# Storing the sums early and adding the expert outputs by accumulating DMAs, in a two-layer attention and mixture-of-experts kernel

## The chip, the cores and the metric

The kernel runs on one core of a Trainium2 chip. The metric is the device time in microseconds, median of several runs of one launch. The engines are TensorE (PE, with its weight loads as PEld), VectorE (DVE), ScalarE (ACT), GpSimd (POOL) and SyncE (SP). SP issues the plain DMAs and POOL the indirect ones, whose row addresses come from a tile of numbers.

## The reference

The input is x with 16 batches of 512 tokens of 128 numbers. Two layers follow; each adds an attention and a feed-forward part to x.

```
xn = layernorm(x)
x = x + cosformer_attention(xn) + moe0(xn)          # 16 experts, top 4, and 2 shared ones
xn = layernorm(x)
x = x + rope_attention(xn) + moe1(xn)
# moe1: 8 experts, each token goes to the one with the highest probability
route = softmax(xn @ router_w + router_b)
for e in range(8):
    a, g = split(xn @ w1[e])                         # w1[e]: 128 x 1024
    y = (silu(a) * g) @ w2[e]                        # w2[e]: 512 x 128
    out = where(argmax(route) == e, y, out)
out = out * max(route)
```

The change touches the last line, the addition of `moe1` to x, and the way in which the result reaches memory.

## The kernel before, in words

**Order.** Each engine runs its own program, and semaphores tie them together. All programs are cut from one list of stages. `placed` gives each stage of a batch a position by hand, in units of which a batch has 20 (`NS`); `stages` sorts all of them by position. So a stage's place in the list decides what stands ahead of it on its engine. The lists `FIRST`, `SECOND` and `ATTENTION` are laid down for each of the 16 batches, and batches overlap. The list `LAST` counts from the last batch.

**Sorting.** As each batch is routed, POOL writes its normalized rows (`sort`, one indirect DMA for 128 rows) into the memory tensor `xs`, each row at a slot of its expert. A row is 129 numbers, 128 values and the token's number. SP later fills the end of each expert's region with 128 rows of zeros marked -1 (`pads`).

**Expert tiles.** `tables` works out which 128 rows and which expert each of 72 tiles has (64 full ones, and up to 8 for the remainders). A tile n has these stages, 1.3 units apart from tile to tile:
- `load` (SP, L1294 and L1295): reads the row address from a table, and brings the tile into one of 4 buffers, `xsb[n % 4]`. The load of tile n+4 waits until tile n has been transposed (`xsT_mm`) and POOL has its row numbers (`rows`).
- `rows` (POOL, L1181 to L1185): three small operations that turn the token numbers into row addresses, with the padding sent to spare rows.
- `turned` (PE L620, ACT L763): the transpose, and its copy to SBUF. `staged` (ACT L757) copies the expert's first weights.
- `hidden` (PE L628, ACT L769, DVE L1076 and L1079): the first product and the gate.
- `outputs` (PE L639): the second product. ACT L774 copies it from PSUM to `ysb`, and POOL L1192 writes it by an indirect DMA to the rows of its tokens in the memory tensor `ys`.

In PE's program the transpose of tile n+1 stands ahead of the first product of tile n and of the second product of tile n-1. The first 20 or so tiles run among the attention of the last batch; the rest run alone.

**The end.** x, with attention and the first layer added, stays in SBUF in the tile `X` until the end (DVE L1021, stage `out`, makes the last addition per batch and counts `x2`). When all rows have arrived in `ys`, SP reads them back in four parts (L1314). DVE multiplies each by the tokens' highest probabilities `pmax` (L1101) and adds it to `X` (L1102), and SP stores it (L1317).

The functions that the change touches follow.

Of the kernel before, what the change touches and what calls it, by code (L numbers as in the profile page):

```python
# [7 lines left out]
ALU = mybir.AluOpType  # L8
# [25 lines left out]
NTAB = NTILE + U  # L34
# [8 lines left out]
K_ID, K_NEG, K_BD, K_TRI, K_ONE, K_SINB, K_COSB, K_RC, K_RS, K_SC, K_BH, K_T, K_E, K_J, K_EYE = range(15)  # L43
WIDTHS = [P, 4 * P, P, P, P, L, L, L, L, 2 * NT, H, NT, 3 * E1 + 1, NTAB, P // 2]
# [3 lines left out]
def constants():  # L48
# [29 lines left out]
    put(K_J, np.arange(NTAB)[None, :])  # L78
    return t
# [30 lines left out]
def placed(**places):  # L110
# [46 lines left out]
    out=[24.55])  # L157
# [3 lines left out]
LAST = [(-19.5, "w1", 0), (-4.5, "w2", 0), (-13, "spares", 0)] + [(-12.4 + 1.2 * k, "tables", k) for k in range(6)]  # L161
# [85 lines left out]
def once(names):  # L247
# [12 lines left out]
    "max heads x2 tables rowzero silu glu chain final "  # L260

    "fills kept ones var0 var1 rstd0 rstd1 qs gated rotated noaT spare nextspare rows xsorted spare_rows "

    "d_x d_w d_restx d_gate d_gates d_relayq d_relayk d_relayed d_sorted d_w1 d_w2 d_pad d_out"
) + [f"d_xs{u}" for u in range(U)] + [f"d_ys{u}" for u in range(U)] + ["d_y"]
# [6 lines left out]
def place(nc, ctx, io):  # L272
# [10 lines left out]
    m.pmax = sb("pmax", [P, B * NT])  # L283
    m.zeros = sb("zeros", [P, D + 1])
# [8 lines left out]
    m.yg = flow[:, :].rearrange("p (t d) -> p t d", d=D)  # L293
# [24 lines left out]
    with ExitStack() as side:  # L318
# [20 lines left out]
        m.xn = [sb(f"xn{n}", [P, NT, D + n], where=side) for n in range(2)]  # L339
# [46 lines left out]
    m.ysb = sb("ysb", [P, U, D])  # L386
# [19 lines left out]

Q = 4
# [384 lines left out]
def vector_program(nc, m, s, order, work):  # L792
# [154 lines left out]
    def expert(b, i):  # L947
# [3 lines left out]
        then(dve.tensor_reduce(m.pmax[:, b * NT:(b + 1) * NT], m.p1[:, :, :], AX_X, ALU.max))  # L951
# [73 lines left out]
    def tables(_, k):  # L1025
# [33 lines left out]
        else:  # L1059
# [4 lines left out]
            then(dve.tensor_scalar(jr[:, 3, :], jr[:, 2, :], float(E1 * CAP), None, ALU.min))  # L1064
# [31 lines left out]

    n = B * NT // Q
    for q in range(Q):
        y, xq = m.yg[:, q * n:(q + 1) * n, :], m.X[:, q * n:(q + 1) * n, :]
        dve.wait_ge(s[f"d_xs{q}"], 16 * (NTILE // U + 2))  # L1100
        then(dve.tensor_tensor(y, y, m.pmax[:, q * n:(q + 1) * n].unsqueeze(2).to_broadcast([P, n, D]), ALU.mult))  # L1101
        dve.tensor_tensor(xq, xq, y, ALU.add).then_inc(s["final"], 1)  # L1102


def pool_program(nc, m, s, order, work):
# [94 lines left out]
    pool.memset(m.zeros[:, D:], -1.0)  # L1200
# [22 lines left out]
def sync_program(nc, m, s, io, order):  # L1223
# [85 lines left out]
    n = B * NT // Q  # L1309
    for u in range(U):  # L1310
# [4 lines left out]
    for q in range(Q):  # L1315
# [65 lines left out]
```

## Time and profile before

| | us |
|---|---|
| median of 3 runs | 1367.89 |
| lowest and highest | 1367.87, 1368.88 |
| span of the profiled execution | 1371.5 |
| PE busy in it | 1209.3 (88%) |
| DVE busy | 991.5 (72%) |
| ACT busy | 912.8 (67%) |
| POOL busy | 692.6 (50%) |

The profile is one execution. Its span, from the first to the last instruction, is its own time, and it is 3.6 us longer than the median. All positions in time below are counted from the span's start. Busy shares are a mean over stages with different limits, so each stage has to be read by itself.

### The profile page before, as it was taken

To read this page: it belongs to the slowest core of one execution; us is meant where nothing else is said; L and a number is where in the kernel's file an instruction comes from. 1 tells how busy PE (TensorE), PEld (TensorE's weight loads), DVE (VectorE), ACT (ScalarE), POOL (GpSimd) and SP (SyncE) were. 2 spreads that over 40 slices of the span, in tenths; PEclk is the share of its full clock that TensorE was granted. 3 is DMA by queue.
4 is the path that set the end of the run, shared out by engine and by line. 5 is a ranking of instruction groups with operands and counts; after the bars stand their busy time and mean duration, and the time that the engine had idled before them with its cause. 6 is when DMAs were issued, how large, how long until landed. Compare 5 with 4: busy or idle time off the path is not lost.

```text
span 1371.5 us, 28942 instructions
## 1 busy us (share of the span) xinstructions
PE 1209.3 (88%) x10216; PEld 700.1 (51%) x10216; DVE 991.5 (72%) x2378; ACT 912.8 (67%) x1233; POOL 692.6 (50%) x1093
## 2 busy tenths in 40 slices
PE   2675999999999999999999999999986999899990
PEld 1342445445454545454454545454432476799990
DVE  2163888888888988888888989888868462344545
ACT  1141777778687868777786877787773667577760
POOL 6324455554536464554545464655543345466760
PEclk9898999999999999999999999999996799999995
DMA  7323505050524416060515335060615210111118
GB/s 224 63 57 64 111 19 115 20 103 27 96 53 71 91 32 120 11 115 20 103 34 88 72 52 105 19 120 14 111 37 171 74 29 25 31 48 50 50 48 250
DMA packets 80300, 100.90 MB, mean 74 GB/s; under 512 B 8800, under 2 KB 56672, under 8 KB 79776
## 3 DMA queue, kind: packets, MB, share of 16 engines
q1 hardware_dynamic: 75680, 89.85, 29.9%
q0 software_dynamic: 4480, 9.22, 2.3%
q8 instruction: 84, 1.38, 0.5%
q14 instruction: 56, 0.46, 0.1%
HBM read 73.50 MB, written 25.01 MB: 72 GB/s over the span
## 4 chain that ended last, share of the span: by engine, by line
PE 63%; DVE 20%; issue 5%; ACT 4%; POOL 4%; DMA 3%; ACTq 0%; SPq 0%; DVEq 0%; POOLq 0%
PE PS L628 9%; PE PS L595 8%; PE PS L440 7%; PE PS L484 7%; PE PS L561 5%; PE PS L639 4%; PE PS L580 4%; PE PS L423 4%; DVE xn L824 3%; PE PS L434 2%; DVE nm L985 2%; DMA early<-gate_rows 2%; PE PS L462 2%; PE PS L570 2%; DVE ra L933 1%
## 5 line engine op out<-in xcount | busy, mean ns | idle before, releaser
L735 ACT ACTIVATE flow<-PS 128x1024 f32<-128x1024 f32 x320 | 321.2, 1028 | 129.4 <-PE PS L580 112.1
L1146 POOL TENSOR_SCALAR_AFFINE_SELECT flow<-flow 128x256 f32<-128x256 f32 (+1 forms) x448 | 191.0, 444 | 374.3 <-ACT flow L735 371.7
L595 PE MATMUL PS<-flow 128*32 128x512 f32 (+3 forms) x2048 | 181.2, 455 | 6.2 <-POOL flow L1146 6.2
L985 DVE TENSOR_REDUCE nm<-PS 128x2 f32<-128x1024 f32 x128 | 154.6, 1220 | 42.3 <-PE PS L549 38.9
L1133 POOL TENSOR_TENSOR early<-early 128x512 f32<-128x512 f32 x128 | 160.7, 1270 | 20.9 <-DMA early<-gate_rows 20.0
L484 PE MATMUL PS<-early,down 128*128 128x512 f32 x288 | 151.8, 637 | 18.4 <-POOL early L1133 17.9
L726 ACT COPY qp<-PS 2x1024 f16<-2x1024 f16 x128 | 128.5, 1004 | 51.0 <-PE PS L570 49.8
L440 PE MATMUL PS<-xnT,up 128*128 128x512 f32 x288 | 152.6, 625 | 3.7 <-DVE at L908 3.4
L987 DVE TENSOR_REDUCE nm<-PS 128x2 f32<-128x768 f32 x128 | 121.6, 950 | 32.4 <-PE PS L549 32.3
L628 PE MATMUL PS<-xsT,w1s 128*128 128x128 f32 x1152 | 141.5, 276 | 3.0 <-DVE act L1079 2.9
L1076 DVE SCALAR_TENSOR_TENSOR tanh<-tanh,PS 128x512 f32<-128x512 f32 x72 | 49.5, 687 | 130.0 <-ACT tanh L769 130.0
L561 PE MATMUL PS<-kp,qp 34*128 34x512 f16 (+3 forms) x1024 | 121.3, 305 | 17.5 <-DVE nm L988 7.8
L628 PEld LDWEIGHTS PS<-xsT,w1s 128*128 128x128 f32 x1152 | 134.5, 192 | 4.3 <-issue 4.1
L667 ACT ACTIVATE early<-PS 128x512 f32<-128x512 f32 x144 | 84.5, 597 | 54.5 <-PE PS L440 53.7
L580 PE MATMUL PS<-qp,kp 34*128 34x512 f16 (+3 forms) x1024 | 114.7, 306 | 5.5 <-ACT flow L735 1.9
L1192 POOL DMA_INDIRECT ys<-ysb,rowu x72 | 76.6, 1063 | 83.2 <-ACT ysb L774 39.2
L561 PEld LDWEIGHTS PS<-kp,qp 34*128 34x128 f16 x1024 | 38.2, 94 | 114.9 <-issue 43.9
L757 ACT COPY w1s<-early 128x1024 f32 x72 | 75.2, 1045 | 23.7 <-issue 23.7
L595 PEld LDWEIGHTS PS<-flow 128*32 128x32 f32 x2048 | 48.6, 110 | 82.1 <-issue 71.1
L580 PEld LDWEIGHTS PS<-qp,kp 34*128 34x128 f16 x1024 | 35.3, 94 | 107.9 <-issue 70.4
L991 DVE TENSOR_REDUCE nm<-PS 128x4 f32<-128x1024 f32 x64 | 78.0, 1219 | 16.3 <-PE PS L549 16.2
L1157 POOL DMA_INDIRECT xs<-xn,slotu x64 | 66.4, 1037 | 39.5 <-DVE slotu L976 29.1
(178 smaller groups left out, 2263.3 us busy)
## 6 DMA issues: line engine op xcount, KB each, us to landing
early<-gate_rows SPq DMA_DIRECT2D x32, 1024.0 KB, 10.8
qp<-relay_q SPq DMA_DIRECT2D x64, 128.0 KB
kp<-relay_k SPq DMA_DIRECT2D x64, 128.0 KB
xsb<-xs SPq DMA_DIRECT2D x76, 64.5 KB, 1.8
relay_k<-qkh SPq DMA_DIRECT2D x32, 128.0 KB, 2.3
early<-in_w SPq DMA_DIRECT2D x1, 4096.0 KB, 14.8
out_y<-X SPq DMA_DIRECT2D x4, 1024.0 KB, 7.9
relay_q<-qkh SPq DMA_DIRECT2D x16, 128.0 KB, 2.3
```

Source lines behind the costliest of these rows:

```text
L440: pe.matmul(ps, m.up[:, c * P:(c + 1) * P], m.xnT[0][:, :], start=True, stop=True).then_inc(s["up_mm"], 1)
L484: pe.matmul(m.acc, m.down[:, c, :], m.hid[:, c, :], start=(c == 0), stop=False)
L561: pe.matmul(ps[:, k, o:o + w], head(m.qp, b, 4 * g + h, slice(qt * P, (qt + 1) * P)), head(m.kp, b, 4 * g + h, slice(0, w)), start=(o == 0 ...
L580: ins = pe.matmul(ps[:, k, o:o + L - kt * P], head(m.kp, b, h, slice(kt * P, (kt + 1) * P)), head(m.qp, b, h, slice(kt * P, L)), start=(o ...
L595: ins = pe.matmul(m.PS[32 * j:32 * j + 32, m.PV, kt * P:], m.vst[b % 2][:, kt, 4 * g + j, :], m.pt[:, r, k * L + o:k * L + o + L - kt * P] ...
L628: ins = pe.matmul(m.PS[:, at + i // FC, i % FC * P:(i % FC + 1) * P], m.w1s[:, n % WS, i * P:(i + 1) * P], m.xsT[:, n % 2, :], start=True, ...
L726: ins = act.copy(m.qp[b % 2][at:at + 2, 2 * g:2 * g + 2, :], ps[at:at + 2, :, :])
L735: act.activation(m.pt[:, n % RING, :], m.PS[:, i:i + 2, :].rearrange("p k c -> p (k c)"), ACT.Exp, scale=1.0 / SCALE).then_inc(s["exp"], 1)
L985: dve.tensor_reduce(nm[:, 3, 2 * n:2 * n + 2], ps, AX_X, ALU.max, negate=True).then_inc(s["max"], 1)
L987: dve.tensor_reduce(nm[:, 2, 2 * n - 4:2 * n - 2], ps[:, :, 0:3 * P], AX_X, ALU.max, negate=True)
L1133: pool.tensor_tensor(m.hid[:, c, :], m.hid[:, c, :], m.gates[:, c - 1, :], ALU.mult).then_inc(s["gated"], 1)
L1146: ins = pool.affine_select(part, part, [[0, part.shape[1]], [1, P]], ALU.is_ge, nothing, base=0, channel_multiplier=-1)
```

## The change

- `xs` rows have 130 numbers: 128 values, the number of the output row, and the highest probability, which DVE writes there at routing. `pmax` is gone.
- The padding rows carry numbers of spare rows at the end of the output and a probability of 0. The spare rows are given a value by one DMA of zeros; the caller cuts them off. So `rows` on POOL is one copy (L1167) instead of three operations, and the stage `spares` is gone.
- The output of a tile is multiplied by the probability as ACT takes it from PSUM, and goes to a slot of `X`, which is free again by then.
- A stage `store` per batch, on SP, writes x of the batch to the output as soon as the sum is made.
- A stage `scatter` on POOL adds a tile's rows to the output rows in memory by an indirect DMA that accumulates. It stands at `max(tile(n + 1) + 0.4, 25 + 0.4 * n)`. The first waits for all stores.
- The load of tile n+4 also waits for tile n's copy from PSUM.
- The read back, the multiplications and additions at the end and the last stores are gone.

```
-LAST = [(-19.5, "w1", 0), (-4.5, "w2", 0), (-13, "spares", 0)] + [(-12.4 + 1.2 * k, "tables", k) for k in range(6)]
+LAST = [(-19.5, "w1", 0), (-4.5, "w2", 0)] + [(-12.4 + 1.2 * k, "tables", k) for k in range(6)]
+    store=[24.8])
+LAST += [(max(tile(n + 1) + 0.4, 25 + 0.4 * n), "scatter", n) for n in range(NTILE)]
...
     def outputs(_, n):
         act.wait_ge(s["yo_mm"], n + 1)
-        act.wait_ge(s[f"d_ys{n % U}"], 16 * (n // U + 1))
-        act.copy(m.ysb[:, n % U, :], wk(("outputs", 0, n))[:, 0:D]).then_inc(s["ycopy"], 1)
+        if n == 0:
+            act.wait_ge(s["d_out"], 16 * (B - 2))
+        if n == FIRSTS:
+            act.wait_ge(s["d_last"], 16 * 2)
+        if n == B * NT:
+            act.wait_ge(s["d_head"], 16 * E1)
+        act.activation(m.X[:, n % (B * NT), :], wk(("outputs", 0, n))[:, 0:D], ACT.Copy,
+                       scale=m.xsb[:, n % U, D + 1:D + 2]).then_inc(s["ycopy"], 1)
...
     def rows(_, n):
         u = n % U
         pool.wait_ge(s[f"d_xs{u}"], 16 * (n // U + 1))
-        pool.wait_ge(s[f"d_ys{u}"], 16 * (n // U + 1))
-        if n:
-            pool.wait_ge(s["nextspare"], n)
-        pool.tensor_scalar(m.isno[:, :], m.xsb[:, u, D:D + 1], 0.0, m.spare[:, 0:1], ALU.is_lt,
-                           ALU.mult).then_inc(s["spare"], 1)
-        pool.wait_ge(s["spare"], n + 2)
-        pool.tensor_scalar(m.rowu[:, u:u + 1], m.isno[:, :], m.xsb[:, u, D:D + 1], None, ALU.add).then_inc(s["rows"], 1)
-        pool.tensor_scalar(m.spare[:, :], m.spare[:, :], float(P), None, ALU.add).then_inc(s["nextspare"], 1)
-
-    def outputs(_, n):
-        u = n % U
+        if n == 0:
+            pool.wait_ge(s["tables"], 1)
+        pool.tensor_copy(m.rowu[:, n:n + 1], m.xsb[:, u, D:D + 1]).then_inc(s["rows"], 1)
+
+    def scatter(_, n):
+        if n == 0:
+            pool.wait_ge(s["d_out"], 16 * (B - 2))
+            pool.wait_ge(s["d_last"], 16 * 2)
+            pool.wait_ge(s["d_spare"], 16)
         pool.wait_ge(s["ycopy"], n + 1)
         pool.wait_ge(s["rows"], n + 1)
         alone()
-        pool.indirect_dma_start(m.ys_d, bass.IndirectOffsetOnAxis(ap=m.rowu[:, u:u + 1], axis=0),
-                                m.ysb[:, u, :], None).then_inc(s[f"d_ys{u}"], 16)
+        pool.indirect_dma_start(m.rows_d, bass.IndirectOffsetOnAxis(ap=m.rowu[:, n:n + 1], axis=0),
+                                m.X[:, n % (B * NT), :], None,
+                                compute_op=ALU.add).then_inc(s["d_head" if n < E1 else "d_added"], 16)
...
     def pads(_, i):
         sp.wait_ge(s["rowzero"], 1)
+        marks = const(m, K_SP).rearrange("p (j c) -> p j c", c=2)
         for e in range(E1):
             row = sp.value_load(m.ti[0:1, 0, e:e + 1], min_val=0, max_val=E1 * CAP - P)
-            sp.dma_start(m.xs_d[bass.ds(row, P), :], m.zeros[:, :]).then_inc(s["d_pad"], 16)
-        sp.dma_start(m.xs_d[E1 * CAP:E1 * CAP + P, :], m.zeros[:, :]).then_inc(s["d_pad"], 16)
+            sp.dma_start(m.xs_d[bass.ds(row, P), 0:D], m.zeros[:, 0:D]).then_inc(s["d_pad"], 16)
+            sp.dma_start(m.xs_d[bass.ds(row, P), D:], marks[:, e, :]).then_inc(s["d_pad"], 16)
+        last = m.xs_d[E1 * CAP:E1 * CAP + E1 * P, :].rearrange("(j p) c -> p j c", p=P)
+        sp.dma_start(last[:, :, 0:D], m.zeros[:, 0:D].unsqueeze(1).to_broadcast([P, E1, D])).then_inc(s["d_pad"], 16)
+        sp.dma_start(last[:, :, D:], marks[:, E1:, :]).then_inc(s["d_pad"], 16)
     def load(_, n):
         if n >= U:
             sp.wait_ge(s["xsT_mm"], n - U + 1)
             sp.wait_ge(s["rows"], n - U + 1)
+            sp.wait_ge(s["ycopy"], n - U + 1)
+    def store(b, i):
+        if b == 0:
+            sp.dma_start(m.spare_d, m.zeros[:, 0:D].unsqueeze(1).to_broadcast([P, NPAD, D])).then_inc(s["d_spare"], 16)
+        sp.wait_ge(s["x2"], b + 1)
+        sp.dma_start(m.out_d[:, b], m.X[:, b * NT:(b + 1) * NT, :]).then_inc(s["d_out" if b < B - 2 else "d_last"], 16)
...
-    for u in range(U):
-        sp.wait_ge(s[f"d_ys{u}"], 16 * (NTILE // U + 1))
-    for q in range(Q):
-        src = m.ys_d[q * n * P:(q + 1) * n * P, :].rearrange("(t p) d -> p t d", p=P)
-        sp.dma_start(m.yg[:, q * n:(q + 1) * n, :], src).then_inc(s[f"d_xs{q}"], 16)
-    for q in range(Q):
-        sp.wait_ge(s["final"], q + 1)
-        sp.dma_start(m.out_d[:, q * B // Q:(q + 1) * B // Q].rearrange("p b t d -> p (b t) d"),
-                     m.X[:, q * n:(q + 1) * n, :]).then_inc(s["d_out"], 16)
-    sp.wait_ge(s["d_out"], 16 * Q)
+    sp.wait_ge(s["d_out"], 16 * (B - 2))
+    sp.wait_ge(s["d_last"], 16 * 2)
+    sp.wait_ge(s["d_spare"], 16)
+    sp.wait_ge(s["d_head"], 16 * E1)
+    sp.wait_ge(s["d_added"], 16 * (NTILE - E1))
```

On POOL, before, each expert tile has the same four instructions: three for its row numbers and the indirect DMA of the tile two before it. At tile 20 they are:

```order
L1192 DMA ys<-ysb,rowu 18176x128 [waits s_ycopy,s_rows]
L1181 TENSOR_SCALAR isno<-xsb,spare 128x1 [waits s_nextspare,s_d_ys3,s_d_xs3]
L1184 TENSOR_SCALAR rowu<-isno,xsb 128x1 [waits s_spare]
L1185 TENSOR_SCALAR spare<-spare 128x1
L1192 DMA ys<-ysb,rowu 18176x128 [waits s_ycopy,s_rows]
L1181 TENSOR_SCALAR isno<-xsb,spare 128x1 [waits s_nextspare,s_d_ys0,s_d_xs0]
```

Now the row copies of tiles 16 to 20 stand alone, and the scatters of the tiles from 0 on follow in groups between the next copies:

```order
L1167 CAST rowu<-xsb 128x1 [waits s_d_xs3]
L1167 CAST rowu<-xsb 128x1 [waits s_d_xs0]
L1177 DMA out_y<-X,rowu 10240x128 [waits s_ycopy,s_rows,s_d_spare,s_d_out,s_d_last]
L1177 DMA out_y<-X,rowu 10240x128 [waits s_ycopy,s_rows] x3
L1167 CAST rowu<-xsb 128x1 [waits s_d_xs1]
L1177 DMA out_y<-X,rowu 10240x128 [waits s_ycopy,s_rows] x3
L1167 CAST rowu<-xsb 128x1 [waits s_d_xs2]
L1177 DMA out_y<-X,rowu 10240x128 [waits s_ycopy,s_rows] x3
```

What moved: the DMA of a tile has left its place two tiles behind. The copies of tiles 21 to 28 stand behind 4, 7, 10, 13, 17, 20, 23 and 26 scatters, and from there on one copy follows each scatter.

On SP, before, only loads stand here, each behind two waits:

```order
L1294 TENSOR_LOAD ji [waits s_rows,s_xsT_mm]
L1294 ISA x2
L1295 ISA
L1295 DMA xsb<-xs 128x129
L1294 TENSOR_LOAD ji [waits s_rows,s_xsT_mm]
```

Now they have three, and the store of the last batch stands between the loads of tiles 23 and 24:

```order
L1284 TENSOR_LOAD ji [waits s_ycopy,s_rows,s_xsT_mm]
L1284 ISA x2
L1285 ISA
L1285 DMA xsb<-xs 128x130
L1291 DMA out_y<-X 128x4x128 [waits s_x2]
L1284 TENSOR_LOAD ji [waits s_ycopy,s_rows,s_xsT_mm]
```

What moved: the store of batch 15 follows the load of tile 23, and the store of batch 14 that of tile 7.

## Rows read from the trace of the kernel before

**Rows 1.** The page, engines' busy time and the span in 40 slices.

```profile
PE 1209.3 (88%) x10216; PEld 700.1 (51%) x10216; DVE 991.5 (72%) x2378; ACT 912.8 (67%) x1233; POOL 692.6 (50%) x1093
...
DMA  7323505050524416060515335060615210111118
```

**Rows 2.** Windows: stretch, length, busy us of each engine, TensorE clock, DMA share, GB/s.

```profile
1033.10:1040.00 6.90, 3.99 (x52) 2.69 (x52) 6.83 (x15) 2.70 (x3) 4.81 (x7) 0.97 1.05 451
1040.00:1050.20 10.20, 5.93 (x50) 2.24 (x54) 7.26 (x21) 3.07 (x3) 5.75 (x9) 0.50 0.36 127
1184.00:1194.00 10.00, 7.17 (x59) 6.70 (x60) 2.99 (x5) 4.42 (x9) 3.85 (x9) 1.00 0.10 28
1305.00:1330.00 25.00, 25.00 (x227) 25.00 (x226) 12.26 (x19) 18.57 (x37) 16.62 (x36) 1.00 0.18 49
1340.00:1350.00 10.00, 0.00 (x0) 0.00 (x0) 3.05 (x2) 0.00 (x0) 0.00 (x0) 0.50 0.74 245
1350.00:1371.50 21.50, 0.00 (x0) 0.00 (x0) 15.01 (x7) 0.00 (x0) 0.00 (x0) 0.50 0.92 279
```

**Rows 3.** Timeline of the end: start, duration, engine, line, operation.

```profile
1337.87 0.27 ACT L774 COPY ysb<-PS 128x128 f32<-128x128 f32 x1 [2.21 <-PE PS L639]
1338.96 0.96 POOL L1192 DMA_INDIRECT ys<-ysb,rowu  x1 [1.41 <-ACT ysb L774]
...
1346.91 2.29 DVE L1101 TENSOR_TENSOR flow<-flow,pmax 128x2048 f32<-128x2048 f32 x1 [10.37 <-DMA flow<-ys]
...
1362.82 2.29 DVE L1102 TENSOR_TENSOR X<-X,flow 128x2048 f32<-128x2048 f32 x1
```

**Rows 4.** SP's longest wait; landing times of L1295, then of L1192.

```profile
SPq L1293 <- POOL rowu L1184: 80.8, 49, 3.3
...
DMA to landing us min/median/max: 1.7/1.8/3.8
...
DMA to landing us min/median/max: 2.3/2.4/4.3
```

**Rows 5.** Timeline of the last tiles, PE, ACT, POOL and SP.

```profile
1326.94 0.27 PE L620 MATMUL PS<-kc,xsb 128*128 128x128 f32 x1
1327.14 0.27 ACT L774 COPY ysb<-PS 128x128 f32<-128x128 f32 x1 [0.30 <-PE PS L639]
1328.84 1.06 PE L639 MATMUL PS<-w,act 128*128 x8
1329.73 0.27 PE L620 MATMUL PS<-kc,xsb 128*128 128x128 f32 x1
1329.79 0.29 POOL L1184 TENSOR_SCALAR rowu<-isno,xsb 128x1 uint32<-128x1 f32 x1
1330.87 0.34 SPq L1295 DMA_DIRECT2D xsb<-xs  x1
```

**Rows 6.** Timeline, tile 19's PSUM copy and tile 32's transpose.

```profile
1191.81 0.27 ACT L774 COPY ysb<-PS 128x128 f32<-128x128 f32 x1 [0.29 <-PE PS L639]
...
1220.96 0.27 PE L620 MATMUL PS<-kc,xsb 128*128 128x128 f32 x1
```

**Rows 7.** DMA issues: tiles, engine, count, KB each, median us to landing.

```profile
X<-in_x SPq DMA_DIRECT2D x1, 256.0 KB, 2.9
```

**Rows 8.** Timeline of POOL, four indirect DMAs in a row.

```profile
1041.20 1.05 POOL L1172 DMA_INDIRECT ys<-zeros,rowu  x1 [0.83 <-POOL rowu L1167]
1042.55 0.97 POOL L1172 DMA_INDIRECT ys<-zeros,rowu  x1 [0.30 <-issue]
...
1045.10 0.97 POOL L1172 DMA_INDIRECT ys<-zeros,rowu  x1 [0.30 <-issue]
```

**Rows 9.** The batches' last sums (L1021), then SP's pads and first loads.

```profile
L1021 DVE TENSOR_TENSOR X<-X,PS x16: 676/677/686, 227.7 to 1183.6; 128x512 f32<-128x512 f32 x16
...
1046.23 8.04 SPq L1283 DMA_DIRECT2D xs<-zeros  x8
1067.93 3.68 SPq L1295 DMA_DIRECT2D xsb<-xs  x4
```

More of the change, by code:

```diff
@@ L33 @@
 U = 4
-NTAB = NTILE + U
+NPAD = 2 * E1
+FIRSTS = B * NT - 2 * NT
+ROW = D + 2
+NTAB = NTILE
 EPS = 1e-5
@@ L78, in constants @@
     put(K_J, np.arange(NTAB)[None, :])
+    spare = B * L + i[:, None] + P * np.arange(NPAD)[None, :]
+    put(K_SP, np.stack([spare, 0 * spare], 2).reshape(P, 2 * NPAD))
     return t
@@ L156 @@
     mT=[22.85],
-    out=[24.55])
-LAST = [(-19.5, "w1", 0), (-4.5, "w2", 0), (-13, "spares", 0)] + [(-12.4 + 1.2 * k, "tables", k) for k in range(6)]
+    out=[24.55],
+    store=[24.8])
+LAST = [(-19.5, "w1", 0), (-4.5, "w2", 0)] + [(-12.4 + 1.2 * k, "tables", k) for k in range(6)]
 LAST += [(-11, "pads", 0)] + [(-5, "load", n) for n in range(U)]
@@ L167, in tile @@
     return TILE0 + STEP * n
-LAST += [(tile(n) + 0.05, "load", n + U) for n in range(NTILE)]
+LAST += [(tile(n) + 0.05, "load", n + U) for n in range(NTILE - U)]
 LAST += [(tile(n - 1) - 0.5, "staged", n) for n in range(NTILE)] + [(tile(n - 1) + 0.3, "rows", n) for n in range(NTILE)]
@@ L259 @@
     "mean0 mean1 norm0 norm1 kvr ks kv px gate at0 x1 xl logits rope low onehot base slots mparts sub0 sub1 "
[L260 to L265, printed above, removed]
+    "max heads x2 tables rowzero silu glu chain "
+    "fills kept ones var0 var1 rstd0 rstd1 qs gated rotated rows "
+    "d_x d_w d_restx d_gate d_gates d_relayq d_relayk d_relayed d_sorted d_w1 d_w2 d_pad d_out d_last d_spare d_added d_head"
+) + [f"d_xs{u}" for u in range(U)]
 class Memory:
@@ L338, in place @@
         m.rstd = sb("rstd", [P, 2, NT], where=side)
-        m.xn = [sb(f"xn{n}", [P, NT, D + n], where=side) for n in range(2)]
+        m.xn = [sb(f"xn{n}", [P, NT, D + 2 * n], where=side) for n in range(2)]
         m.xnT = [sb(f"xnT{n}", [P, L], where=side) for n in range(2)]
@@ L372, in place @@
     m.tf = sb("tf", [P, 6, E1 + 1])
-    m.spare = sb("spare", [P, 1])
-    m.isno = sb("isno", [P, 1])
-    m.rowu = sb("rowu", [P, U], U32)
+    m.rowu = sb("rowu", [P, NTILE], U32)
     m.jr = sb("jr", [P, 4, NTAB])
     m.ji = sb("ji", [P, 3, NTAB], I32)
-    m.xsb = sb("xsb", [P, U, D + 1])
+    m.xsb = sb("xsb", [P, U, ROW])
     m.xsT = sb("xsT", [P, 2, P])
@@ L405 @@
 NW = 13
-Q = 4
 def tensor_program(nc, m, s, order, work):
@@ L950, in expert @@
         dve.tensor_reduce(m.s1[:, 3, :], m.p1[:, :, :], AX_X, ALU.max)
-        then(dve.tensor_reduce(m.pmax[:, b * NT:(b + 1) * NT], m.p1[:, :, :], AX_X, ALU.max))
+        then(dve.tensor_reduce(m.xn[1][:, :, D + 1], m.p1[:, :, :], AX_X, ALU.max))
         desc = m.kc[:, int(KO[K_E]) + E1:int(KO[K_E]) + 2 * E1].unsqueeze(1).to_broadcast([P, NT, E1])
@@ L1063, in tables @@
                                           op0=ALU.mult, op1=ALU.add))
-            then(dve.tensor_scalar(jr[:, 3, :], jr[:, 2, :], float(E1 * CAP), None, ALU.min))
+            then(dve.tensor_scalar(jr[:, 3, :], jr[:, 2, :], float(E1 * CAP + (E1 - 1) * P), None, ALU.min))
             then(dve.tensor_scalar(jr[:, 0, :], jr[:, 0, :], float(E1 - 1), float(2 * F1), ALU.min, ALU.mult))
@@ L1191, in outputs @@
         alone()
-        pool.indirect_dma_start(m.ys_d, bass.IndirectOffsetOnAxis(ap=m.rowu[:, u:u + 1], axis=0),
-                                m.ysb[:, u, :], None).then_inc(s[f"d_ys{u}"], 16)
-    share = dict(stats0=stats0, stats1=stats1, q=q, gated=gated, score=scores, rope=rope, sort=sort, spares=spares, rows=rows,
-                 outputs=outputs)
+        pool.indirect_dma_start(m.rows_d, bass.IndirectOffsetOnAxis(ap=m.rowu[:, n:n + 1], axis=0),
+                                m.X[:, n % (B * NT), :], None,
+                                compute_op=ALU.add).then_inc(s["d_head" if n < E1 else "d_added"], 16)
+    share = dict(stats0=stats0, stats1=stats1, q=q, gated=gated, score=scores, rope=rope, sort=sort, rows=rows,
+                 scatter=scatter)
     nothing = pool.to_reg(0.0)
@@ L1293, in load @@
             sp.wait_ge(s["rows"], n - U + 1)
-        row = sp.value_load(m.ji[0:1, 2, n:n + 1], min_val=0, max_val=E1 * CAP)
+            sp.wait_ge(s["ycopy"], n - U + 1)
+        row = sp.value_load(m.ji[0:1, 2, n:n + 1], min_val=0, max_val=E1 * CAP + (E1 - 1) * P)
         sp.dma_start(m.xsb[:, u, :], m.xs_d[bass.ds(row, P), :]).then_inc(s[f"d_xs{u}"], 16)
-    share = dict(gT=gT, parts=parts, relay=relayed, w1=w1, w2=w2, pads=pads, load=load)
+    def store(b, i):
[3 more added lines that the diff above has]
+        sp.dma_start(m.out_d[:, b], m.X[:, b * NT:(b + 1) * NT, :]).then_inc(s["d_out" if b < B - 2 else "d_last"], 16)
+    share = dict(gT=gT, parts=parts, relay=relayed, w1=w1, w2=w2, pads=pads, load=load, store=store)
     sp.dma_start(m.X[:, 0:NT, :], m.x_d[:, 0]).then_inc(s["d_x"], 16)
@@ L1345, in build @@
           for n, s, d in _INS}
-    io["out"] = nc.dram_tensor("out_y", [B, L, D], F32, kind="ExternalOutput").ap()
+    io["out"] = nc.dram_tensor("out_y", [B * L + NPAD * P, D], F32, kind="ExternalOutput").ap()
     program(nc, io)
```

39 lines of the change are left out of this document (9 added, 30 removed).

## The prediction

> **What bounds the kernel now.** I read four views, in this order. The page gives TensorE 88% of the span [rows 1], and the stages say where that stops being true [rows 2]. In the expert stage (1305 to 1330) PE is busy 25.00 of 25.00 us, DVE 12.26, ACT 18.57, POOL 16.62. From 1340 to the end PE, ACT and POOL do nothing. DVE works 18.1 us of that and the DMA engines run at 0.74 and 0.92 of their time. So there are two pieces: a stage bound by PE at one tile per 2.79 us (transposes L620 at 1326.94 and 1329.73 [rows 5]), and a serial tail behind it.
>
> The tail in order [rows 3]: the last indirect store is issued at 1338.96, the rows come back into SBUF, DVE multiplies and adds from 1346.91 to 1365.11, the stores follow, and the span ends at 1371.5. That is 32.5 us after the last indirect store's start, and nothing in it overlaps PE.
>
> Then the loop that feeds PE. A tile's load is issued by SP, which waits 80.8 us over 49 times for POOL's row numbers L1184 [rows 4]. The row numbers end at 1330.08 and the DMA starts at 1330.87: 0.8 us from semaphore to DMA [rows 5]. It lands after 1.7/1.8/3.8 us (min/median/max) [rows 4]. So the gate of a load has to open 0.8 + 1.8 = 2.6 us before PE transposes that tile. SP and POOL look idle, but they sit in the path of every load.
>
> **Tail: removed.** The read back and 8 DVE operations go, and 4 MB of stores move ahead. What is left behind the last tile is one scatter. It starts at 1338.96 as before, since it waits for the same PSUM copy, and must land. The plain one lands after 2.3/2.4/4.3 us [rows 4]. An accumulating one must also read its rows first; no row shows that. The bounds are 2.3 below and 4.8, twice the median, above. I take 3.3, nearer the plain row since the bytes are few. Saved: 32.5 - 3.3 = 29.2 us (27.7 to 30.2).
>
> **POOL's queue: the burst.** The scatters may not start before batch 15's sum is stored, and the order puts none before position 25. In POOL's program 4 scatters stand between the row copies of tiles 20 and 21, then 3 before each next copy (4 once), until 26 scatters are out ahead of tile 28's copy. Tile n+4's load waits for tile n's copy, so these scatters stand in front of PE's food.
> - Start: store 15 stands on SP behind load 23, which now waits for tile 19's PSUM copy, ending at 1192.08 [rows 6]. Plus 0.8 to that load, 0.4 to issue it, 2.9 for 256 KB to land (as the 256 KB of x from in_x do [rows 7]): 1196.2. The first scatter starts 0.8 later, as POOL's start behind a copy does (ysb ends 1337.87 + 0.27, DMA 1338.96 [rows 3]): 1197.0.
> - Pitch: four indirect DMAs in a row, of which rows 8 has three, start 1.35 us apart at first and (1045.10 - 1042.55) / 2 = 1.27 after [rows 8]; I take 1.30. Serial with its wait it would be 0.82 + 1.06 = 1.88, the upper bound if an accumulating one costs POOL what a plain one does. Below is 1.27.
> - 26 scatters take 33.8 us, 8 row copies at 0.3 (L1184, 0.29 [rows 5]) 2.4 us. Tile 28's copy ends at 1233.2; plus 2.6, tile 32 can be transposed at 1235.8. Before, that was 1220.96 [rows 6]. PE loses 14.8 us. At 1.27 it loses 14.0, at 1.88 it loses 29.9. After that POOL has one scatter and one copy per tile, 1.6 us of 2.8, and catches up in about three tiles.
>
> The step is on the path, not beside it: by tile 25 the copy comes at about 1202.3, the transpose at 1204.9, 3.5 us late, and PE has nothing else in its queue.
>
> **The new wait on the PSUM copy.** The output now is scaled by a number that lies in the loaded tile, so load n+4 must also wait for tile n's PSUM copy. Before, for the last tile: tile 67's copy ends at 1327.41 (1327.14 + 0.27) and tile 71 is transposed at 1329.73, 2.32 us later [rows 5]. 2.6 is needed, so it is 0.28 late. In full: from a transpose to the end of the next output product is 2.96 us (1326.94 to 1329.90), the copy ends 0.30 after that, then 2.6: 5.86 us for two tiles where it was 5.58. That is 0.14 per tile; 38 tiles (34 to 71): 5.3 us. Lower bound 0, should the chain be 0.3 shorter; upper 10, should a load land 0.25 later beside accumulating traffic. Queued behind the waiting load on SP are only the next loads and store 15. The tiles run among attention (0 to 23) have slack and pay nothing.
>
> **Clock.** Between 1033.1 and 1040.0 PE was busy 3.99 of 6.90 us, 0.58, and the granted clock was then 0.50 (1.2 GHz); between 1184 and 1194 it was busy 0.72 and kept 1.00 (2.4 GHz) [rows 2]. In the burst a tile takes 3 x 1.30 + 0.3 = 4.2 us for 2.8 of work, 0.66, between the two. At the low level a tile's 2.8 us becomes up to 5.6, 1.4 more than POOL allows. Such stretches hide partly under the burst. I take 1.0 us (0 to 6).
>
> **Costed at nothing.** Stores 0 to 13 are 256 KB each, some 64 us apart (16 sums from 227.7 to 1183.6 [rows 9]), and the DMA engines are half busy or less in most slices [rows 1]; no load or relay stands close behind them on SP. The 18 pad DMAs that replace 9 take SP 8 x (1.1 + 0.4) + 0.8 = 12.8 us from 1046.2, to 1059; the first load stood at 1067.93 (9 us of cover) [rows 9]. The spare stores that go (1041.20 to 1046.07 on POOL) stood beside a DVE-bound stretch (7.26 of 10.20): a gain of 0 to 1. The scaled copy is an ACTIVATE instead of a COPY; both run at like rates here (tanh, 512 columns, 0.60; w1s, 1024, 1.05), and ACT has 6 of 25 us free. The one multiply and two additions fewer in POOL's row numbers shorten nothing that is waited for once the PSUM copy is the later gate.
>
> **Sum.** -29.2 + 14.8 + 5.3 + 1.0 = -8.1. The profiled execution's span is 1371.5 and it would be 1363.4. The median of the three runs is 1367.9, 3.6 lower; I carry the difference over: 1359.8.
>
> **A rule weighed.** Four plain indirect DMAs show 1.27 to 1.35 us of pitch [rows 8], and each keeps POOL 0.97 to 1.05 us. The Trainium skill, page "Collectives: The Full Stack" (The bandwidth ceiling), says that a DMA reduce needs two read descriptors for each write, so that read traffic doubles, while the add itself costs nothing. No row here shows an accumulating DMA. By that rule POOL, which writes these descriptors, may need up to twice its time, and the sum would end above the time before; by the row it needs the same, and the sum is -8.1. Rival A has this as a mechanism of this kernel, in rows.
>
> **Rivals.**
> - *A: an accumulating scatter keeps POOL longer, slower than before.* If POOL's part grows from 1.06 to twice that, the pitch is 2.4 and 26 scatters take 62 us: tile 32 at 1264, 43 us late, and the sum is near +20: 1388. It decides from a pitch of 1.61 (1.30 plus 8.1/26). A pitch of 1.88 gives +7, 1375. For: nothing shows how such a DMA is issued, and 26 of them multiply every tenth by 2.6 us. Against: every plain one here takes the same 1.0 to 1.1.
> - *B: the PSUM copy's wait costs nothing.* Loads land in 1.7, the chain holds in 2.32: -13.4, 1354.5. For: 1.7 is the minimum row. Against: 0.8 of SP's time stands in every load.
> - *C: POOL's burst stays hidden and only the tail counts:* -29, 1339. It needs row copies ahead of the scatters, and POOL's order says otherwise.
> - *D: as forecast, but PE runs cold in the burst or accumulates slow the loads* by 6 to 8 us more: no change, 1366 to 1369.
>
> **How the numbers follow.** Forecast (1355 to 1364.5): 0.42. B (1349 to 1355): 0.13. C: 0.05. D (1364.5 to 1370.6): 0.14. A: 0.26. This kernel's measurement tells 0.2% (2.7 us), so faster is below 1365.2: 0.42 + 0.13 + 0.05 + 0.01 of D = 0.61. Same, to 1370.6: 0.13. Slower: 0.26. The range leaves out C and the far half of A: 1349 to 1378. Where signs are mixed, the forecast's own range is 1355 to 1364.5.
>
> **What would show it.** Indirect DMAs on POOL from about 1197, 1.3 us apart, row copies between them waited for by SP; transposes 4.2 us apart from tile 25 to 32; after that 2.93 instead of 2.79, with PE idle before the transpose and released by the load; the last scatter near 1359 of the span and the end 3.3 later. I am wrong if DMA_INDIRECT takes clearly more than 1.1 us, if PE stays full after 1240, or if the transposes keep 2.79 through the burst.

## The result and the profile after

| | us |
|---|---|
| changed kernel, median of 4 | 1381.77 (1378.83 to 1386.70) |
| before, median of 4 beside it | 1368.39 (1367.87 to 1370.34) |
| ratio | 1.0094, 95% interval 1.0067 to 1.0122 |
| span of the profiled execution | 1377.4 |

The change makes the kernel slower by 0.9%, some 13 us. The forecast was 1359.8 us. All the same its largest term came as worked out: the tail is 29 us shorter. But 42 us were lost ahead of it. Of all executions behind the times in this document one was in a slow state, the fifth of e2 (3915.1 us), and the ratios leave it out.

The page of the changed kernel: busy times, clock and DMA in 40 slices, and the software DMA queue, which carries POOL's indirect DMAs:

```profile
PE 1225.3 (89%) x10216; PEld 710.8 (52%) x10216; DVE 966.7 (70%) x2370; ACT 919.9 (67%) x1233; POOL 679.2 (49%) x942
...
PE   2676999999999999999999999999976899768997
...
PEclk9887999999999999999999999999996899979999
DMA  7333607052432606051533516050553100243333
...
q0 software_dynamic: 12416, 8.99, 5.2%
```

The last slices of DMA are 3 where they were 1 and, at the very end, 8 [rows 1]: the burst of read back and stores has gone. PE is less than full in slices 35 to 37 (1171 to 1274); in slice 36 the granted clock is 0.7.

Windows of the changed kernel (as in [rows 2]): the two halves of the burst of scatters, and the steady expert stage behind it.

```profile
1189.00:1213.00 24.00, 16.54 (x116) 15.67 (x115) 6.82 (x10) 10.48 (x19) 20.01 (x16) 0.84 0.42 42
1213.00:1237.00 24.00, 15.60 (x98) 14.73 (x97) 5.50 (x8) 8.89 (x16) 20.62 (x18) 0.78 0.44 46
1300.00:1325.00 25.00, 23.38 (x200) 22.29 (x200) 11.07 (x17) 17.50 (x33) 14.12 (x16) 1.00 0.34 44
```

Two losses, both new. In the burst PE has 32.1 of 48 us and POOL 40.6: POOL is the bound, since between its DMAs it is idle for only 0.3 us each. In the steady stage, where PE was busy 25.00 of 25.00, it now has 23.38 with no other engine full: a chain with a wait in it. Who waits over the whole span, first PE before its transposes, then SP before its loads (engine, line waited for: us, times, longest):

```profile
PE PS L621 <- DMA xsb<-xs: 25.5, 26, 4.6
```

```profile
SPq L1283 <- ACT X L780: 174.3, 59, 23.5
...
SPq L1283 <- POOL rowu L1167: 39.9, 8, 6.5
```

The load was gated by the row number [rows 4]. Now the PSUM copy ends its wait 59 times and the row copy 8 times. The eight are the burst's. Of the 59, 21 lie before it, among the attention, where the transposes come no later for it (tile 24's comes 15.4 us after the last attention sum, and 15.1 before the change); 38 lie behind it.

POOL and SP in the burst: the store of batch 15 and the first scatter, then one step of the burst.

```profile
1186.53 0.43 SPq L1291 DMA_DIRECT2D out_y<-X  x1
1189.77 1.64 POOL L1177 DMA_INDIRECT out_y<-X,rowu  x1 [16.37 <-ACT X L780]
```

```profile
1204.87 1.55 POOL L1177 DMA_INDIRECT out_y<-X,rowu  x1 [0.30 <-issue]
1206.72 1.55 POOL L1177 DMA_INDIRECT out_y<-X,rowu  x1 [0.30 <-issue]
1207.71 0.77 POOL L1167 CAST rowu<-xsb 128x1 uint32<-128x1 f32 x1
1208.63 1.57 POOL L1177 DMA_INDIRECT out_y<-X,rowu  x1 [0.16 <-POOL rowu L1167]
1210.50 1.55 POOL L1177 DMA_INDIRECT out_y<-X,rowu  x1 [0.30 <-issue]
```

An accumulating indirect DMA keeps POOL 1.56 us where the plain one takes 0.96 to 1.05 [rows 3, 8]. With the 0.30 behind it the pitch, the time from one start to the next, is 1.85 to 1.87. The row copy starts at 1207.71, before the scatter ahead of it ends (1206.72 + 1.55 = 1208.27), and the next scatter comes 1.91 after that one: its 0.77 us lie under the scatter but for 0.04. So one tile's row copy comes every three scatters, 3 x 1.87 = 5.6 us, while PE needs 2.8 us for a tile.

PE's transposes of tiles 26, 32, 34 and 71 (tile 32 is to be compared with [rows 6], tile 71 with [rows 5]):

```profile
1205.57 0.33 PE L621 MATMUL PS<-kc,xsb 128*128 128x128 f32 x1 [0.15 <-DMA xsb<-xs]
...
1241.08 0.33 PE L621 MATMUL PS<-kc,xsb 128*128 128x128 f32 x1 [0.93 <-DMA xsb<-xs]
...
1247.19 0.33 PE L621 MATMUL PS<-kc,xsb 128*128 128x128 f32 x1 [0.30 <-DMA xsb<-xs]
...
1364.83 0.33 PE L621 MATMUL PS<-kc,xsb 128*128 128x128 f32 x1 [0.58 <-DMA xsb<-xs]
```

Tile 32 to 71 took 1329.73 - 1220.96 = 108.8 us before [rows 5, 6] and takes 123.8 now. From 34 to 71 it is 117.64 / 37 = 3.18 us a tile, where it was 2.79. And tile 32 is 20.1 us later, though this execution was 6.8 us ahead at the last attention sum (1176.8 against 1183.6 [rows 9]), so 26.9 us are lost up to there.

The end, last PSUM copy and last scatter (to be compared with [rows 3]):

```profile
1373.03 0.37 ACT L780 ACTIVATE X<-PS,xsb 128x128 f32<-128x128 f32 x1 [2.10 <-PE PS L640]
1374.22 1.54 POOL L1177 DMA_INDIRECT out_y<-X,rowu  x1 [0.93 <-ACT X L780]
```

The span ends at 1377.4, 3.2 us after the last scatter's start, where it was 32.5. The account from the two traces: +26.9 up to tile 32, +15.0 from tile 32 to 71, +0.2 from there to the last scatter, -29.3 in the tail: +12.8. The medians say +13.4.

### The profile page after: what moved, and what is told of

It reads as the page before. It is cut to its first block and busy times, and to the rows that moved or that the text cites. A ratio compares the mean times of both kernels' runs of the same rounds, so it can differ in the third digit from the quotient of the medians.

```text
span 1377.4 us, 28645 instructions
## 1 busy us (share of the span) xinstructions
PE 1225.3 (89%) x10216; PEld 710.8 (52%) x10216; DVE 966.7 (70%) x2370; ACT 919.9 (67%) x1233; POOL 679.2 (49%) x942
## 3 DMA queue, kind: packets, MB, share of 16 engines
q0 software_dynamic: 12416, 8.99, 5.2%
HBM read 69.09 MB, written 26.30 MB: 69 GB/s over the span
## 5 line engine op out<-in xcount | busy, mean ns | idle before, releaser
L1177 POOL DMA_INDIRECT out_y<-X,rowu x72 | 112.4, 1562 | 79.7 <-ACT X L780 67.7
L629 PE MATMUL PS<-xsT,w1s 128*128 128x128 f32 x1152 | 148.7, 285 | 2.1 <-DVE act L1086 2.1
L629 PEld LDWEIGHTS PS<-xsT,w1s 128*128 128x128 f32 x1152 | 140.9, 200 | 3.4 <-issue 3.1
L1157 POOL DMA_INDIRECT xs<-xn,slotu x64 | 66.1, 1033 | 39.6 <-DVE slotu L983 29.2
```

The source lines that it names most:

```text
L629: ins = pe.matmul(m.PS[:, at + i // FC, i % FC * P:(i % FC + 1) * P], m.w1s[:, n % WS, i * P:(i + 1) * P], m.xsT[:, n % 2, :], start=True, ...
```

## The experiments

The kernel before was run beside each group, and the ratios are to that median: 1368.39 us beside the changed kernel, 1369.56 beside e1 to e4, 1369.88 beside e0 and e5 to e7, 1368.46 beside e8 to e11. The time of a run is the median of four executions (of five for e2 and e10, one for e0). Differences in the text are of these medians as they stand; by the ratios they come out up to 2.3 us otherwise.

| run | us | ratio (95%) |
|---|---|---|
| changed kernel | 1381.77 | 1.0094 (1.0067 to 1.0122) |
| e1 plain scatter | 1382.35 | 1.0092 (1.0067 to 1.0118) |
| e2 row number on DVE | 1360.56 | 0.9941 (0.9919 to 0.9963) |
| e3 probability copied out on POOL, no PSUM-copy wait | 1357.78 | 0.9916 (0.9894 to 0.9938) |
| e4 both on DVE, no such wait | 1339.42 | 0.9774 (0.9751 to 0.9797) |
| e5 row number by another operation | 1383.78 | 1.0099 (1.0078 to 1.0120) |
| e6 8 load buffers | 1358.82 | 0.9915 (0.9893 to 0.9936) |
| e7 as e4, plain | 1340.21 | 0.9787 (0.9768 to 0.9807) |
| e8 as e6, plain | 1342.02 | 0.9809 (0.9793 to 0.9825) |
| e9 as e2, 5 buffers | 1337.68 | 0.9773 (0.9758 to 0.9788) |
| e10 as e4, 8 buffers | 1339.49 | 0.9784 (0.9767 to 0.9800) |
| e11 as e2, plain | 1359.13 | 0.9937 (0.9920 to 0.9954) |

**e2_rows_dve: the row number off POOL.** The stage `rows` moves with its wait to DVE's program.

```
-        pool.tensor_copy(m.rowu[:, n:n + 1], m.xsb[:, u, D:D + 1]).then_inc(s["rows"], 1)
...
+        dve.tensor_copy(m.rowu[:, n:n + 1], m.xsb[:, u, D:D + 1]).then_inc(s["rows"], 1)
```

> The row-number copy of each tile runs on DVE instead of POOL; the loads still wait for the PSUM copy. Theory (burst of scatters ahead of the row copies holds the loads): the transposes keep their steady pitch of about 3.18 us from tile 24 on and never show 5.6, which takes 39 - 24 = some 20 us out; span about 1354 to 1358, time about 1357. POOL still issues its scatters 1.87 us apart but nobody waits for it. Rival (the accumulating traffic itself starves the loads or the clock falls anyway): the pitch between tiles 24 and 33 stays above 4 us and less than 8 us is gained.

Measured: 1360.56 us, 21.2 less than the changed kernel. The scatters still come 1.86 us apart, but no tile waits for them. Its transposes (1195.0 for tile 24, 1345.6 for tile 71 in the timeline) are 3.20 us apart on average, and no step is above 4.7. So the burst has left PE's path, and the other loss has not.

**e3_scale_pool: the wait for the PSUM copy taken away.** The probability is copied out of the loaded tile by POOL, ACT scales from there, and a load no longer waits for ACT.

```
+        act.wait_ge(s["rows"], n + 1)
...
-                       scale=m.xsb[:, n % U, D + 1:D + 2]).then_inc(s["ycopy"], 1)
+                       scale=m.top1[:, n:n + 1]).then_inc(s["ycopy"], 1)
...
+        pool.tensor_copy(m.top1[:, n:n + 1], m.xsb[:, u, D + 1:D + 2])
...
-            sp.wait_ge(s["ycopy"], n - U + 1)
```

> POOL also copies each tile's probability out of the load buffer (one more copy of 128x1 per tile), ACT takes it from there, and the load of tile n+4 no longer waits for the PSUM copy of tile n. Theory (that wait costs 15 us over the 38 tiles after the burst): pitch after tile 34 is 2.79 instead of 3.18, the burst is 9 x 0.3 to 0.8 = 3 to 7 us longer; time about 1368 to 1372. Rival (the steady loss is the accumulating DMAs' or the clock's): the pitch stays near 3.1 and the time at 1379 or above.

Measured: 1357.78 us, 24.0 less than the changed kernel. A gain of 10 to 14 was expected. Windows of e3, burst and steady stage:

```profile
1200.00:1225.00 25.00, 15.55 (x103) 14.60 (x101) 5.50 (x8) 8.41 (x17) 21.62 (x22) 0.86 0.43 46
...
1300.00:1325.00 25.00, 25.00 (x227) 25.00 (x226) 12.28 (x18) 19.46 (x37) 16.96 (x27) 1.00 0.37 48
```

The steady stage is full again; the burst stands. Part of the gain is an earlier burst: store 15 no longer waits behind a waiting load, and the first scatter starts at 1180.60 in place of 1189.77, with the last attention sum at 1176.8 in both traces.

**e4_both_dve: both edits.** The two copies of e3 stand on DVE.

> Row number and probability are both copied out by DVE, and the loads do not wait for the PSUM copy. Theory (burst on the path and the wait on the PSUM copy are the whole of the loss): PE is full from tile 24 on at 2.79 us per tile, POOL's 72 scatters at 1.87 us end by about 1324, before the last tile, and only the 29 us of the tail count; time about 1338 to 1342. Rival (accumulating traffic slows the loads by itself): a pitch of 2.9 to 3.1 and 1345 to 1355.

Measured: 1339.42 us. Windows of e4, the burst (two rows) and the steady stage:

```profile
1200.00:1225.00 25.00, 25.00 (x227) 25.00 (x226) 13.40 (x37) 19.48 (x37) 21.03 (x14) 1.00 0.49 60
1225.00:1250.00 25.00, 25.00 (x227) 25.00 (x226) 13.27 (x37) 19.39 (x37) 21.00 (x14) 1.00 0.50 63
1300.00:1325.00 25.00, 25.00 (x227) 25.00 (x226) 13.40 (x37) 19.59 (x36) 14.01 (x9) 1.00 0.35 47
```

PE is full while POOL, at 21 of 25 us, works off the same scatters beside it. Against the kernel before, run beside it, 30.1 us are gained (1369.6 - 1339.4). The traces say where 29.1 of them are: from the last attention sum to tile 71's transpose it takes 146.1 us in both (1183.6 to 1329.7 before, 1181.0 to 1327.1 in e4), so nothing is lost there, and from that transpose to the end 12.6 us in place of 41.8, 29.1 less. The four times make a square: the row copy on POOL costs 1357.8 - 1339.4 = 18.4 us without the wait and 21.2 with it; the wait costs 1360.6 - 1339.4 = 21.2 on DVE and 24.0 on POOL. Each of the two alone would have eaten most of the tail's gain. Together they turn it into a loss.

**e1_plain: scatters that store plainly** (it leaves out the addition).

```
-                                m.X[:, n % (B * NT), :], None,
-                                compute_op=ALU.add).then_inc(s["d_head" if n < E1 else "d_added"], 16)
+                                m.X[:, n % (B * NT), :], None).then_inc(s["d_head" if n < E1 else "d_added"], 16)
```

> The 72 scatters are plain instead of accumulating (this leaves out the addition of the expert output to the stored sums, the output rows are overwritten); everything else is the changed kernel. Theory (an accumulating scatter keeps POOL 1.56 us where a plain one keeps it 1.06, and 26 of them stand in front of a row copy): DMA_INDIRECT falls to about 1.06 us, their pitch from 1.87 to about 1.35, tile 32 is transposed 26 x 0.5 = 13 us earlier, and if accumulating traffic also slows the loads, the steady pitch falls from 3.18 to about 3.0. Time about 1360 to 1367. Rival (the pitch is set by the waits of the scatter, not by the addition): DMA_INDIRECT stays near 1.5 us and the time within 3 us of 1379.

Measured: 1382.35 us, a miss. DMA_INDIRECT fell to 0.98 us and the pitch to 1.27, yet the time did not move. Timeline of e1_plain, PE and ACT in the middle of the burst:

```profile
1205.07 0.27 PE L629 MATMUL PS<-xsT,w1s 128*128 128x128 f32 x1 [0.35 <-issue]
1205.77 0.27 PE L629 MATMUL PS<-xsT,w1s 128*128 128x128 f32 x1 [0.43 <-issue]
...
1206.49 0.36 PE L629 MATMUL PS<-xsT,w1s 128*128 128x128 f32 x1 [0.45 <-issue]
...
1208.60 0.37 PE L629 MATMUL PS<-xsT,w1s 128*128 128x128 f32 x1 [1.75 <-issue]
...
1212.89 0.60 ACT L770 ACTIVATE tanh<-PS 128x512 f32<-128x512 f32 x1 [13.95 <-remote]
...
1222.73 0.37 ACT L780 ACTIVATE X<-PS,xsb 128x128 f32<-128x128 f32 x1 [9.25 <-remote]
```

From 1204 to 1225 PE gets out a few matmuls, one at a time at first, and what it waits for is "issue", nothing that the profile shows. The transposes of tiles 25 and 26 are 23.7 us apart. This hole, as it is called below, confounds the test: it neither bears out nor refutes the pitch. e7, e8 and e11 were made to get around it.

One thing e1 does show is what the addition costs in the software queue:

```profile
q0 software_dynamic: 4352, 8.99, 2.2%
```

It has the same bytes in 4352 packets, 32 for each of the 64 sorting DMAs and 72 scatters, where the changed kernel has 12416. So an accumulating scatter takes 144 packets, four and a half times the plain one's 32.

**e7_plain_dve and e11_plain_rows_dve: plain scatters with the row number on DVE**, without the wait (e7) and with it (e11). Both leave out the addition.

> As e4_both_dve (row number and probability copied out on DVE, no wait for the PSUM copy; 1339 us), but the scatters store plainly instead of adding; it leaves out the addition of the stored sums. Theory: plain scatters issued back to back (pitch 1.28 us) hold up the other engines' instruction streams, which made the 25 us hole of e1_plain: then a hole stands here too, 1355 to 1365 us. Rival: the hole of e1_plain came from its row copies on POOL and the waits behind them: then 1337 to 1340 us, 2.79 us a tile throughout.

> e1_plain with the row number written on DVE, the wait for the PSUM copy kept; it leaves out the addition. If the hole of e1_plain needs row copies behind scatters on POOL: no hole, 3.1 to 3.2 us a tile, 1355 to 1360 us. If it needs only the wait for the PSUM copy beside plain scatters back to back: hole again, near 1380 us.

Measured: e7 1340.21 us (e4: 1339.42), e11 1359.13 (e2: 1360.56). No hole in either, so my theory that plain scatters at a pitch of 1.27 hold up the other engines by themselves is false. They tell two more things. With the row number off POOL's queue it makes no difference whether a scatter costs POOL 0.96 or 1.56 us, nor that the DMA engines are busy 0.35 of the time with accumulating scatters (e4, 1300 to 1325) and 0.17 with plain ones (e7). And e11 keeps 3.1 to 3.2 us a tile (PE 23.43 of 25 us from 1300 on) without any accumulating traffic, so that is not the cause of the second loss.

**e5_rows_ts: the same row number by another operation.** The copy (CAST in the trace) shows 0.78 us, while a TENSOR_SCALAR on the same engine showed 0.29 before [rows 5].

```
-        pool.tensor_copy(m.rowu[:, n:n + 1], m.xsb[:, u, D:D + 1]).then_inc(s["rows"], 1)
+        pool.tensor_scalar(m.rowu[:, n:n + 1], m.xsb[:, u, D:D + 1], 0.0, None, ALU.add).then_inc(s["rows"], 1)
```

> The changed kernel with the row number written by a tensor_scalar (add 0) on POOL in place of tensor_copy. If the copy's own 0.78 us is part of each 5.6 us step of the burst: the copy takes 0.3 us, a step 5.1 to 5.2 us, 9 steps give back 4 to 5 us, so about 1377 us. If the step is set by something else (scatters alone, or the loads): no difference, 1381 to 1382 us.

Measured: 1383.78 us, no gain. Timeline of POOL in e5's burst:

```profile
1213.96 1.56 POOL L1177 DMA_INDIRECT out_y<-X,rowu  x1 [0.30 <-issue]
1214.98 0.81 POOL L1167 TENSOR_SCALAR rowu<-xsb 128x1 uint32<-128x1 f32 x1
1215.95 1.58 POOL L1177 DMA_INDIRECT out_y<-X,rowu  x1 [0.17 <-POOL rowu L1167]
```

The tensor_scalar takes 0.81 here and starts inside the scatter. Its minimum elsewhere in this run is 0.21, and a CAST behind a plain scatter took 0.20 (e1). So the 0.8 us belong to the place behind an accumulating scatter, not to the operation, and they cost nearly nothing, as they overlap it.

**e6_buf8: 8 load buffers in place of 4**, nothing else changed.

```
-U = 4
+U = 8
```

> The changed kernel with 8 load buffers in place of 4. Theory: both costs are one chain, a load waits for work four tiles back (row copy in the burst, scaled PSUM copy after it). Then with eight the transposes follow row copies 8 tiles back: transpose 36 comes where transpose 32 came (1241), 12 us gained; after it 2.79 us a tile in place of 3.18, 14 us gained over 35 tiles; together about 1355 us. Rival: the steady 3.18 is set by ScalarE (activation with scale, 0.37 us against 0.27 us of a copy) or by the transfers of the accumulating stores: then only the burst's part comes back, about 1369 us.

Measured: 1358.82 us, 23.0 less; the theory said about 1355, the rival 1369. Windows of e6, burst and steady stage:

```profile
1225.00:1250.00 25.00, 16.55 (x104) 15.79 (x104) 5.49 (x8) 9.03 (x17) 21.77 (x20) 0.80 0.45 48
1300.00:1325.00 25.00, 25.00 (x227) 25.00 (x226) 12.28 (x19) 19.58 (x36) 15.78 (x20) 1.00 0.39 49
```

The steady stage is full with the activation's scale and the accumulating stores unchanged. So the second loss was the depth of the chain, four buffers. The burst only ends four tiles later (tile 36's transpose in place of tile 32's) with five transposes held up in place of eight, and PE still has 16.55 of 25 us in it.

**e8_plain_buf8: e6 with plain scatters** (it leaves out the addition).

> e6_buf8 (8 load buffers, 1359 us) with scatters that store plainly; it leaves out the addition of the stored sums. Theory: what e6 still loses is the pitch of the accumulating scatter (1.87 us, three to a row copy on POOL); with plain ones (pitch 1.27) the row copies come 3.8 us apart and 8 buffers cover them nearly: about 1340 to 1343 us, if the 25 us hole of e1_plain does not come. Rival: the hole comes with plain scatters whenever row copies wait behind them on POOL: then 1355 to 1365 us.

Measured: 1342.02 us, 16.8 less than e6. Here the hole of e1 is absent, and the pitch can be read. Windows of e8 over the same stretch:

```profile
1225.00:1250.00 25.00, 24.14 (x217) 23.95 (x217) 11.49 (x17) 18.95 (x35) 17.29 (x30) 1.00 0.26 74
```

PE has 24.14 us where e6 had 16.55. That is the price of 0.6 us more per scatter when row copies stand behind 26 of them: 26 x 0.6 = 15.6, and 16.8 was measured (14.5 by the ratios). That the accumulating traffic costs nothing by itself, e4 and e7 have shown.

**e9_dve_buf5: e2 with one more buffer.** U = 5.

> e2_rows_dve (row number on DVE, the load still waits for the scaled PSUM copy; 1361 us, 3.20 us a tile) with 5 load buffers in place of 4. Theory: 3.20 us is a chain of 12.8 us over four tiles; over five it is 2.56 us a tile, under PE's own 2.79, so 2.79 us a tile: 1339 to 1342 us. Rival: something else makes the 3.20 us (ScalarE's longer activation, the accumulating stores' transfers): little change, 1357 to 1361 us.

Measured: 1337.68 us. Two transposes in the steady stage of e9:

```profile
1318.50 0.27 PE L621 MATMUL PS<-kc,xsb 128*128 128x128 f32 x1
1321.29 0.27 PE L621 MATMUL PS<-kc,xsb 128*128 128x128 f32 x1
```

They are 2.79 us apart again. The wait for the PSUM copy is still there and one buffer hides it. This version and e4 beat both kernels; which of them is the faster these runs do not tell.

**e10_both_buf8: e4 with 8 buffers.**

> e4_both_dve (1339 us) with 8 load buffers. Theory: PE has no idle time left in the expert stage (2.79 us a tile), so nothing is gained: 1338 to 1341 us. Rival: more loads ahead of the stage cover the few late transposes before tile 24: 1334 to 1337 us.

Measured: 1339.49 us. Nothing to gain: PE was full already.

**e0_before: the kernel before, profiled once more.**

> The kernel before, unchanged, profiled once more. Theory: the profile read for the prediction was an execution some 4 to 5 us longer than most, and the difference lies ahead of the expert stage; here the last attention output sum (batch 15) comes near 1177 us in place of 1183.6 and transposes of tiles 24 to 71 keep 2.79 us. Rival: x2 of batch 15 at 1183 again: the change made the attention stage 6 us shorter.

Measured: one execution of 1370.16 us, span 1368.4; DVE's sum of batch 15 at 1181.7. A miss on both sides. The same sum came at 1183.6 in the profile used for the prediction. In the twelve traces with the change in some form it lies between 1176.8 (changed kernel) and 1184.9 (e6), in the mean at 1179.9. So it moves by up to 8 us from trace to trace, and positions after it are compared only after taking this off, as done above. Whether the change also made the part ahead of it 2 to 3 us shorter, two traces of the kernel before do not tell.

## Why the prediction was wrong

The sign was wrong and the sum was off by 22 us. Its steps:

- **Tail, -29.2: right.** Measured -29.3. The span ended 3.2 us after the last accumulating scatter's start; I had taken 3.3.
- **Start of the burst: right.** Predicted at 1197.0, measured at 1189.77, in an execution that was 6.8 us ahead: 1196.6 on the scale of before. Store 15 did stand behind a load that waits for a PSUM copy.
- **Pitch, the step that failed most.** I took 1.30 us, the row of plain stores, and 1.88 only as an upper bound. That bound was meant for a scatter that waits serially. 1.87 came for another reason, that the DMA itself takes 1.56; that it meets the bound is luck. 26 x 1.87 = 48.6 us against my 33.8 + 2.4 = 36.2, 12.4 more. Predicted loss to tile 32: 14.8, measured 26.9. Rival A had the mechanism, with 1.61 as the point from which it decides and 1375 us at a pitch of 1.88, and I weighed it too lightly. What the 0.6 us of pitch are worth by themselves e8 shows for 8 buffers: 16.8 us. For 4 buffers no run shows it, because of e1's hole; there it rests on the rows, in which the held transposes come 5.5 to 5.75 us apart behind three scatters and 7.5 to 7.6 behind four.
- **The rule weighed.** The rule cited from the Trainium skill ("Collectives: The Full Stack", The bandwidth ceiling), two read descriptors for each write, pointed the right way for POOL's time, which rose from 0.98 (e1) to 1.56 us, by six tenths and not to the double that I drew from it as the far case. The profile's counts do not show the doubled reads: the software queue has 8.99 MB with plain and with accumulating scatters, and the page has 69.09 MB read from HBM in both. What grew is the packets, from 32 to 144 a scatter.
- **Row copies, 2.4: wrong, small.** They add 0.04 us each, since they lie under the scatter ahead of them.
- **PSUM-copy wait, 5.3: mis-sized, the other half of the miss.** From tile 34 on a tile took 3.18 us, not 2.93; against the 2.79 of before that is 14.4 us for 37 tiles. The chain had the right links. Mean links over the last 22 tiles of the changed kernel, counted in the trace: transpose to the end of the PSUM copy two tiles back 3.41 (I had 3.26), to the load's DMA 0.83 (0.8), to the transpose 2.02 (1.8). Together 6.26 for two tiles against 5.86. 0.10 is the ACTIVATE, 0.37 us where the COPY took 0.27 [rows 5], which I had costed at nothing; 0.22 is the load, which I took at its median landing. My 0.28 was the small difference of two numbers near 5.8, so small errors in the links more than doubled it. Without the burst the tiles from 24 on pay it too, 47 and not 38: e2 and e4 differ by 21.2 us.
- **Clock, 1.0: nothing of its own.** The granted clock fell to 0.84 and 0.78 on average in the two halves of the burst, after PE had been idle between tiles. Still tile 32's transpose starts 2.62 us after tile 28's row copy ends (1238.46), which is the load's time alone: PE waits for the row copy, and a slower matmul only fills that wait. It shows in the busy time. PE is busy 16.0 us longer than before (1225.3 against 1209.3), and these with the 25.5 us of idle before transposes are 41.5 of the 42 us lost. In e4, where PE never waits, it is busy 1209.3 again.
- **Rivals B, C and D** are refuted for this kernel: the wait cost 15 us and not 0, the burst was not hidden, and what was lost was not lost to the clock or to slower loads (the loads land after 1.7/1.8/2.8 us, min, median and max, no later than before [rows 4]). C's number, 1339, is what e4 and e9 reach once row copies are off POOL and the wait is gone or covered.

With the measured pitch and my wait the sum is -29.3 + 26.9 + 5.3 = +3; with my pitch and the measured wait it is -29.3 + 15.8 + 15.0 = +1.5. Either miss alone made it no gain; only both make the 13 us.

What stays open is the hole of e1_plain. It came with plain scatters, row copies behind them on POOL, and 4 buffers; with the row number on DVE (e7, e11) or 8 buffers (e8) it did not. The rows say only that PE, ACT and DVE had nothing to issue, and that between 1203 and 1224 the software queue was the only one that moved anything. What held the instructions back stays open, and the account of e1's time with it.

## What to carry to other kernels

When stores are moved out of a serial tail, look at what stands behind them in the queue of the engine that issues them. Small work that feeds the bound engine must not be there: here a 0.2 us copy moved to another engine is worth 21 us. When a new reader keeps a buffer longer, write down the whole loop through the buffers and ask for a margin of one buffer, not for equality; one more buffer of 520 bytes a partition was worth another 23 us. And an operation that no row shows should be priced in the forecast by its bad end if dozens of them stand in series. Another remedy for the first loss, an order of POOL's list with fewer scatters ahead of each row copy, was not tried.

## What the runs showed of the hardware

- An accumulating indirect DMA of 128 rows of 512 bytes keeps POOL 1.56 us (1.54 to 1.64), a plain one of the same rows 0.95 to 0.99 (e1, e7, e8). Pitch back to back 1.85 to 1.87 and 1.27. Packets 144 and 32.
- It is soon done all the same: the span ends 3.2 us (changed kernel) and 3.3 us (e4, last scatter 1336.4, span 1339.7) after the last one's start.
- POOL's instruction behind an accumulating scatter shows 0.76 to 0.82 us in place of 0.2 and starts 0.5 to 0.6 us before that scatter's end (changed kernel, e5). A duration in a row is not always a cost: here the step time tells, not the row.
